# Routing the first layer's tokens in three groups instead of two, between the last attention tiles

## What is computed

```python
h = _layernorm(x) * (1 + ca) + sa
x = x + ga * _L0_attn_ref(h, ...)              # causal softmax attention, per batch
h = _layernorm(x) * (1 + cb) + sb
# _L0_ffn_ref:
logits = x_flat @ router_w.T                    # N = 2048 rows, E = 8 experts
chosen_e = argmax(softmax(logits)); chosen_p = max(softmax(logits))
pos = cumsum(onehot(chosen_e), axis=0)[row, chosen_e] - 1     # place in its expert's queue
kept = pos < C                                  # C = 384
buf[chosen_e, pos] += x_flat * kept             # rows scattered into expert slots
h = gelu(buf @ w1 + b1); eo = h @ w2 + b2       # per expert
y = eo[chosen_e, pos] * (chosen_p * kept)       # gathered back
x = x + gb * y
```

## Time and profile before

| | us |
|---|---|
| median of 3 runs | 942.2 (939.58 to 942.33) |
| the profiled execution: time | 943.0 |
| its span, first to last instruction | 941.3 |
| PE busy | 900.4 (96%) |
| ACT busy | 642.7 (68%) |
| DVE busy | 580.4 (62%) |
| POOL busy | 307.0 (33%) |
| mean granted clock of PE, of full speed | 0.98 |

### The profile page before, as it was taken

One profiled execution on the slowest core, in us unless ns is written; L12 is line 12 of the kernel. 1 busy time (PEld: TensorE's weight loads), 2 busy tenths in 40 slices (PEclk: granted clock), 3 DMA queues, 4 the chain that ended last, 5 costly groups with the idle time before them and its releaser, 6 DMA issues.

```text
span 941.3 us, 25419 instructions
## 1 busy us (share of the span) xinstructions
PE 900.4 (96%) x10209; PEld 662.7 (70%) x10209; DVE 580.4 (62%) x1348; ACT 642.7 (68%) x1094; POOL 307.0 (33%) x393
## 2 busy tenths in 40 slices
PE   8999995599999999999999999999999999999988
PEld 5687684366777777767777777767677776777777
DVE  5557011685666666666666666666666666667795
ACT  3552332487788787887878788787887878787343
POOL 4233802533423223241423223232424232325220
PEclk9998898799999999999999999999999999999999
DMA  8400622100020002002000200110020002000001
GB/s 238 163 2 23 198 99 56 31 2 2 2 94 2 3 6 90 2 2 94 2 3 1 94 3 1 58 38 2 2 94 1 2 2 42 2 2 2 1 12 34
DMA packets 27128, 35.48 MB, mean 38 GB/s; under 512 B 6042, under 2 KB 21716, under 8 KB 26836
## 3 DMA queue, kind: packets, MB, share of 16 engines
q1 hardware_dynamic: 25988, 31.76, 10.2%
q0 software_dynamic: 1024, 2.10, 0.8%
HBM read 28.48 MB, written 5.37 MB: 36 GB/s over the span
## 4 chain that ended last, share of the span: by engine, by line
PE 88%; DVE 5%; issue 2%; ACT 2%; DMA 1%; POOL 1%; SPq 0%; DVEq 0%; ACTq 0%; POOLq 0%
PE CX L444 24%; PE SC L407 19%; PE PT L427 15%; PE MI L388 6%; PE MI L386 3%; PE CX L463 2%; PE SC L1667 2%; PE PT L1678 2%; PE SC L1762 2%; PE SC L1528 1%; PE CX L1776 1%; PE MI L463 1%; PE SC L1444 1%; PE PT L1538 1%; PE MI L1551 1%
## 5 line engine op out<-in xcount | busy, mean ns | idle before, releaser
L566 DVE CUSTOM_DVE_ANT_0 soft<-SC,strips 128x1024 f32<-128x1024 f32 x256 | 303.3, 1222 | 76.8 <-PE SC L407 76.8
L527 ACT ACTIVATE soft<-soft,nmax 128x1024 f32<-128x1024 f32 x256 | 294.2, 1150 | 1.9 <-DVE nmax L566 1.9
L444 PE MATMUL CX<-PTs,V 128*64 128x256 f32 x2048 | 246.2, 383 | 0.0
L512 ACT COPY PTs<-PT 128x1024 f32<-128x1024 f32 x128 | 129.6, 1013 | 134.7 <-PE PT L427 134.7
L407 PE MATMUL SC<-qk 64*128 64x512 f32 x1536 | 209.5, 404 | 3.2 <-DVE nmax L566 1.5
L444 PEld LDWEIGHTS CX<-PTs,V 128*64 128x64 f32 x2048 | 143.3, 137 | 93.3 <-issue 36.1
L427 PEld LDWEIGHTS PT<-ident,soft 64*128 64x128 f32 x4096 | 158.5, 138 | 68.0 <-issue 28.2
L574 DVE COPY PTs<-PT 128x512 f32<-128x512 f32 x128 | 88.6, 692 | 159.8 <-PE PT L427 159.8
L427 PE MATMUL PT<-ident,soft 64*128 64x64 f32 x4096 | 175.6, 225 | 2.7 <-ACT PTs L512 2.4
L407 PEld LDWEIGHTS SC<-qk 64*128 64x128 f32 x1536 | 135.8, 186 | 27.3 <-issue 1.9
L613 POOL TENSOR_TENSOR x<-x,wo_out 128x256 f32<-128x256 f32 x64 | 47.5, 742 | 206.8 <-DVE wo_out L583 206.8
(11 more groups left out here) (281 smaller groups left out, 991.5 us busy)
## 6 DMA issues: line engine op xcount, KB each, us to landing
strips<-bias_vec SPq DMA_DIRECT2D x8, 1920.0 KB, 8.6
arena<-in_L_ffn_w SPq DMA_DIRECT2D x1, 2048.0 KB, 12.3
slots_in<-arena SPq DMA_DIRECT2D x1, 1536.0 KB, 8.6
arena<-slots_in SPq DMA_DIRECT2D x8, 192.0 KB, 3.7
slots_out<-arena SPq DMA_DIRECT2D x8, 192.0 KB, 2.1
x<-in_L_attn_x SPq DMA_DIRECT2D x2, 512.0 KB, 4.3
out<-x SPq DMA_DIRECT2D x4, 256.0 KB, 2.3
arena<-in_L_wmod SPq DMA_DIRECT2D x2, 384.0 KB, 5.3
```

The costliest lines, as they stand in the source:

```text
L444: ins = pe.matmul(CX[hd * DK:(hd + 1) * DK, 0:2 * P], V1[:, vb, t, hd * DK:(hd + 1) * DK], PTs[:, g % 2, hd, t, :], start=(t == 0), stop=( ...
L512: act.copy(turned_out(n, 0), turned_in(0)).then_inc(ev("ptA_out"), 1)
L527: act.activation(soft[:, n % RING, hd, :], soft[:, n % RING, hd, :], ACT.Exp, bias=nmax[:, j:j + 1], scale=-1.0, accum_out=rsum[:, hd, n % ...
L566: dve.tensor_tensor_reduce(soft[:, n % RING, hd, :], SC[hd][:, :], strips[:, u // B % 2, hd, i * P:i * P + S], 1.0, 3.4e38, ALU.add, ALU.m ...
```

## The change

The router works in three groups, tiles 0 to 7, 8 to 11 and 12 to 15 (`group`), and each has its own logits, choice, ranks, slot numbers and scatter. The order of attention tiles becomes 0 to 7, then 11 to 8, then 15 to 12, so that group 1 is complete after place 11; places 8 to 15 have widths 4, 3, 2, 1, 8, 7, 6, 5. Group 0's choice, ranks and slot numbers are written between the last attention places. POOL modulates group 0's rows in 16 operations of one tile each, where it used two of eight tiles. DVE modulates groups 1 and 2, each behind other work. Banks are reassigned, the last two attention places are written out of the loops, and PE's filler is 16 and 6 dummies (before 16, 5 and 6) and the 30 ahead of the experts, as before.

```diff
-        vec_banks = [PT[0], SC[0][:, 0:512], PT[1], SC[1][:, 0:512]]
+        vec_banks = [PT[0], PT[1], SC[0][:, 0:512], SC[1][:, 0:512]]
...
+
+        logit_banks = [SC[1][:, 0:64], SC[0][:, 0:32], MI[:, 0:32]]
+        rank_banks = [SC[1][:, 64:128], SC[0][:, 64:96], CX[:, 0:32]]
...
+        def group(g):
+
+            return (tiles(0), quarter(2), quarter(3))[g]
...
-        order0 = list(range(TB)) + list(range(NT - 1, TB - 1, -1))
+        order0 = list(range(TB)) + [11, 10, 9, 8] + [15, 14, 13, 12]
...
-                return four_sc[(3, 1, 0, 2)[k]]
+                return four_sc[(0, 1, 3, 1)[k]]
...
-            link(pool.tensor_tensor(rows_mod[:, tiles(0), :], rows0[:, tiles(0), :], bc_tiles(mod[:, 0, 0, 2, :], TB), ALU.mult))
-            link(pool.tensor_tensor(rows_mod[:, tiles(0), :], rows_mod[:, tiles(0), :], bc_tiles(mod[:, 0, 0, 1, :], TB), ALU.add))
+            for t in range(TB):
+                ins = pool.tensor_tensor(rows_mod[:, t, :], rows0[:, t, :], mod[:, 0, 0, 2, :], ALU.mult)
+            link(ins)
+            for t in range(TB):
+                ins = pool.tensor_tensor(rows_mod[:, t, :], rows_mod[:, t, :], mod[:, 0, 0, 1, :], ALU.add)
+            link(ins)
             pool.wait_ge(ev("slots_zeroed"), 16)
             scatter(0)
-            pool.wait_ge(ev("rows_mod_ready"), 1)
-            scatter(1)
+            for g in (1, 2):
+                pool.wait_ge(ev("rows_mod_ready"), g)
+                scatter(g)
...
-                if i == 14:
-                    norm_out(1, (0,))
+            turned0(NT - 4)
+            norm_out(1, (0,))
+            exp0(NT - 2)
+            turned0(NT - 3)
+            exp0(NT - 1)
+            turned0(NT - 2)
+            norm_out(1, (1,), (0,))
+            turned0(NT - 1)
...
-                if j % TB == TB - 1:
+                if j in (7, 11, 15):
                     link(ins)
-                    norm_variance(1, j // TB)
+                    variance_of(group((7, 11, 15).index(j)))
...
+            def group_rows(g):
+
+                link(tt(rows_mod[:, group(g), :], rows0[:, group(g), :], bc_tiles(mod[:, 0, 1, 2, :], 4), ALU.mult))
+                tt(rows_mod[:, group(g), :], rows_mod[:, group(g), :], bc_tiles(mod[:, 0, 1, 1, :], 4),
+                   ALU.add).then_inc(ev("rows_mod_ready"), 1)
+
+            def group_norm(g):
+
+                dve.wait_ge(ev("var_ready"), batches_until(1, g))
+                inverse_roots(group(g))
...
-            for i in range(4, NT):
+            for i in range(4, NT - 1):
+                if i == 13:
+                    dve.wait_ge(ev("inverse_ready"), 1)
+                    rows_out(tiles(0), rows0)
...
-                if i == 12:
-                    dve.wait_ge(ev("inverse_ready"), 1)
-                    rows_out(tiles(0), rows0)
+            stats0(NT - 5)
+            group_norm(1)
+            added0(NT - 4)
+            biased0(NT - 1)
+            router_choice(0)
+            rows_out(group(1), rows0)
+            slot_places(0)
+            added0(NT - 3)
             stats0(NT - 4)
-            router_choice(0)
-            added0(NT - 3)
             stats0(NT - 3)
+            dve.wait_ge(ev("h_ready"), 7)
+            dve.wait_ge(ev("mod0_ready"), 1)
+            group_rows(1)
             added0(NT - 2)
             stats0(NT - 2)
-            slot_places(0)
             added0(NT - 1)
             stats0(NT - 1)
-            dve.wait_ge(ev("var_ready"), batches_until(1, 1))
-            inverse_roots(tiles(1))
-            rows_out(tiles(1), rows0)
-            dve.wait_ge(ev("h_ready"), 8)
-            dve.wait_ge(ev("mod0_ready"), 1)
-            link(tt(rows_mod[:, tiles(1), :], rows0[:, tiles(1), :], bc_tiles(mod[:, 0, 1, 2, :], TB), ALU.mult))
-            tt(rows_mod[:, tiles(1), :], rows_mod[:, tiles(1), :], bc_tiles(mod[:, 0, 1, 1, :], TB), ALU.add).then_inc(ev("rows_mod_ready"), 1)
+            group_norm(2)
+            rows_out(group(2), rows0)
             router_choice(1)
             slot_places(1)
-            for b in range(B):
-                slot_weights(b)
+            router_choice(2)
+            slot_places(2)
+            dve.wait_ge(ev("h_ready"), 8)
+            group_rows(2)
+            for g in range(3):
+                slot_weights(g)
...
-            def logits0(b):
-
-                bank = (PT[1], MI)[b]
-                pe.wait_ge(ev("hT_ready"), 4 + 2 * b + 2)
-                if b == 0:
-                    pe.wait_ge(ev("pt0_out"), 12)
...
+                bank, some = logit_banks[g], group(g)
+                pe.wait_ge(ev("hT_ready"), 6 + g)
+                if g < 2:
+                    pe.wait_ge(ev("nmax0"), NT - 1 + g)
...
-                else:
+                pe.wait_ge(ev("hot_ready"), g + 1)
+                if g == 2:
                     pe.wait_ge(ev("att0_out"), NT)
...
-            for i in range(4, NT + 3):
-                if i < NT:
-                    scores0(i)
-                if 5 <= i < NT + 2:
+            for i in range(4, NT - 1):
...
                     turn0(i - 2)
-                if i >= 5:
                     context0(i - 3)
-                if i == 13:
-                    turn_rows(1, 0)
-                    turn_rows(1, 1)
-                if i == 15:
-                    logits0(0)
-                if i == 17:
-                    ranks0(0)
+            pe.wait_ge(ev("nmax0"), NT - 2)
+            turn_rows(1, 0)
+            turn_rows(1, 1)
+            turn0(NT - 3)
+            context0(NT - 4)
+            logits0(0)
+            pe.wait_ge(ev("hT_ready"), 6)
+            scores0(NT - 1)
+            turn0(NT - 2)
+            context0(NT - 3)
+            turn_rows(1, 2)
+            ranks0(0)
+            turn0(NT - 1)
+            context0(NT - 2)
+            context0(NT - 1)
+            logits0(1)
             def bias_columns(k):
 
...
             bias_columns(1)
-            keep_clock(four_sc[3], 16)
-            pe.wait_ge(ev("vec_ready"), 2)
-            turn_rows(1, 2)
-            keep_clock(four_sc[3], 5)
+            pe.wait_ge(ev("att0_out"), NT - 1)
+            keep_clock(CX, 16)
             turn_rows(1, 3)
-            keep_clock(four_sc[3], 6)
-            logits0(1)
+            keep_clock(CX, 6)
+            logits0(2)
             ranks0(1)
-            pe.wait_ge(ev("slot_numbers"), 1)
+            ranks0(2)
+            pe.wait_ge(ev("slot_numbers"), 2)
             bias_columns(2)
             bias_columns(3)
...
             pe.wait_ge(ev("scattered"), 16 * NT)
-            pe.wait_ge(ev("slot_numbers"), 2)
+            pe.wait_ge(ev("slot_numbers"), 3)
```

More of the change, by code:

```diff
@@ L751, in inverse_roots, with scatter @@
                 ins.then_inc(ev("inverse_ready"), 1)
-            def scatter(b):
-                pool.wait_ge(ev("slot_numbers"), b + 1)
-                for t in range(b * TB, b * TB + TB):
+            def scatter(g):
+                pool.wait_ge(ev("slot_numbers"), g + 1)
+                for t in range(group(g).start, group(g).stop):
                     pool.indirect_dma_start(slots_in, bass.IndirectOffsetOnAxis(ap=slot_s[:, t:t + 1], axis=0),
@@ L1581, in ranks0 @@
+                for t in range(some.stop):
+                    at = max(t - some.start, 0)
+                    mm(bank[:, at * E:], ones, hot1b[:, t:t + 1, :].to_broadcast([P, n - at, E]),
                        start=False, stop=False, skip_group_check=True)
[L1582 removed]
+                ins = mm(bank, before, hot1b[:, some.start + 1:some.stop + 1, :].rearrange("p t e -> p (t e)"), start=False, stop=True,
```

103 lines of the change are left out of this document (51 added, 52 removed).

## The result

| | us |
|---|---|
| before, median of 15 runs | 942.2 (939.58 to 943.07) |
| after, median of 15 runs | 945.06 (941.39 to 948.0) |
| ratio | 1.0036, 95% interval 1.0025 to 1.0048 |
| profiled execution of after | 947.21, span 945.5 (before 943.0, 941.3) |

What follows compares the result with a forecast made beforehand. Before, the scatter ended the stage; after, PE's own row of small work was to bound it. Slots 3.2 us later less 1.9 saved entering the experts gave +1.3, so 942.2 becomes 943.5, range 939.3 to 947.5.

Steps and rivals of the forecast that it cites:

- PE's own row: Group 2's ranks, bias, modulation and thirty dummies ahead of the experts: becomes the bound, ending at 110.3, +3.2 on 107.06.
- rival A: Clock falls in the attention's tail after PE's idle times, adding 1.5 and 1.7 us: 946.7, slower; chance 31%.
- Prices and the narrow places: Per-width costs in attention 0; narrow places 8 to 10 save PE 3.0 us ahead of batch 0's variance.
- The knot: Batch 0's eight row tiles ahead of wide place 13 in DVE's order: PE idles 2.5 us until 64.2.
- Slot numbers of batch 0: End of batch 0's router: 78.3 against 78.12 before, so moved up in order but not in time.
- the last addition: End of DVE's additions for the last attention places: 81.8 against 78.65 before, +3.1.
- The sixteen dummies: PE's dummies after group 0's bias matmuls: 3.6 us at 2.4 GHz or 5.2 as before, ending 86.5 or 88.1.
- Group 1's ranks: Queued behind group 2's logits on PE, ending 89.7 or 91.3; DVE waits 1.6 to 3.2 us for them.
- POOL: Idle 2.7 to 4.3 us between its two scatter blocks; last issue ends at 102.1 or 103.7, against 103.09.
- The warm entry: PE enters the experts straight from its dummies without the idle 1.60, saving 1.9 us in the first block.
- the 1.7 us in the thirty dummies: Extra cost in the dummies ahead of the experts if the clock comes back only there.
- Rival C: POOL's tile-wise operations hold DVE's root chain of group 1, ending about 71; at most 0.5 added: 944.0; chance 5%.

Runs made afterwards that it cites:

- yardstick: The changed kernel itself run once more with no edit, on a slow chip; 952.71 against 948.73 for before, ratio 1.0042.
- ranks first: After, with group 1's ranks moved ahead of group 2's row transposes, six dummies and logits in PE's order; 949.35, ratio 1.0007 to before.
- knot: After, with place 13's biased step moved ahead of batch 0's eight row tiles in DVE's order; 949.52, ratio 1.0005 to before.
- best: After, with place 13 ahead of the rows, fewer dummies, group 1's ranks earlier and modulation vectors as filler; 944.4 against 948.73, ratio 0.9948 to before.
- best, again: A second run of the version with all four edits to after, on the same slow chip; 943.37 against 949.21 for before, ratio 0.9946.
- after, 14 dummies: After, with 14 in place of 30 dummy matmuls ahead of the experts; 948.61 against 949.41 for before, ratio 0.9995.
- after, filler: After, with 9 and 8 dummy matmuls put into PE's two idle times in the attention's tail; 950.65, ratio 1.0017 to before.
- before, 14 dummies: The kernel before, with 14 in place of 30 dummy matmuls ahead of the experts; 949.21, ratio 1.0002 to before.

## Why the prediction was right, and where its working was not

The forecast was 943.5 with 939.3 to 947.5, most of the chance on a difference under 0.3%. The median came out 1.5 us above it, within the range and just over the edge of what was called the same (0.36%). The direction and the bound were right: PE's own row replaces the scatter, as the chain shows, and no profile of the changed kernel or its variants has PE waiting for the slots. The size was not: +1.3 us forecast, +2.9 measured, and the forecast's ratio of 1.0014 lies outside the interval of 1.0025 to 1.0048. The forecast's own range, 941.5 to 945, just misses the median; the stated range holds it because rival A stretches it to 947.5.

- **Prices and the narrow places.** Batch 0's variance was forecast at 55.5 and came at 55.08; roots done at 59.6, came at 59.2. Right.
- **The knot.** PE idle 2.5 us until 64.2 forecast; 2.27 until 63.83 measured. Its removal moved the tail by 1.9 us.
- **Slot numbers of batch 0.** 78.3 forecast, 79.36 measured; the last addition 81.8, measured 83.3. The steps were right, their clock was not: in 65.5 to 68.5 and 79 to 82 it was 0.50. Against the yardstick, which had the full clock there, each of the two stretches cost 1.4 us, at row transposes, transposes and contexts. (Two of the sums on the way were 0.2 too high each: 71.6 and 4.07 make 75.7, and 75.9 and 2.2 make 78.1.)
- **The sixteen dummies.** Forecast from 82.9 to 88.1 at the latest, measured from 85.4 to 90.7. Their own time was priced right (5.2, the slow end I took); it is their start that was 2.5 late, and 2.4 of it was there when the last contexts ended (82.7 in place of 80.3). This is the term that was too small, and what it left out is the lower clock in the attention's tail, which the forecast put at nothing and only rival A priced. Group 1's ranks ended at 93.8 and not 91.3, and DVE's wait for them was 4.32 in place of 3.2.
- **POOL.** Gap forecast 2.7 to 4.3, measured 4.86. The last issue was to end at 103.7 and ended at 105.5.
- **PE's own row.** From the one-hot to the end of the dummies I counted 15.4 us at the lower clock and 0.85 more. It took 16.3 (96.35 to 112.63). So the row was priced right and began 2.3 us late: slots at 112.63 against 110.3.
- **The warm entry.** 1.9 forecast, 1.7 measured.
- **Rival A**, the clock falling in the attention's tail, is what the profiled execution shows, at 31% of the chance and 946.7 where that execution took 947.2. It priced the fall behind PE's second idle time; there was one behind the first, too. The closeness of the sum is luck: of its terms the 1.7 us in the thirty dummies did not come (7.00 us against 6.86), and the two falls together cost 2.8 where 1.5 was taken. On another chip the tail kept the full clock and the ratio was the same, since the row waited there for something else. On the chip where before takes 942, the kernel with group 0's rows in two operations, otherwise after, had one such stretch and not two, and its profiled execution took 944.9. Of the fifteen executions of after the fastest (941.4) has the highest mean granted clock, 0.983, and the two slowest (947.9 and 948.0) 0.974. So the clock explains the profiled 4.2 against 1.3 and part of the spread; how much of the median's 2.9 it is is not shown.
- **Rival C** was seen in part: DVE's chain took 0.85 us more and ended at 69.6, where I had it end at about 71, and DVE had no scores before 73.1, so that nothing of it reached the time. The Trainium skill, "SBUF — State Buffer", Who interferes with whom, limits the blocking to DVE instructions with two SBUF inputs or in a two-port mode. The rows agree for L1090 and L1091. L1087 and L1088 have one input and took 0.38 as well; they are tensor_scalar, which that section names among the operations that can enter a two-port mode. Whether they ran in it no run here shows.

The three engines form a circle: group 1's ranks, behind group 2's logits in PE's list, hold DVE, which holds group 2's one-hot, which holds PE's row. The working had it (91.3, 92.5, 94.0), and its steps came out as counted: 93.8, 94.9, 96.35. Through this circle the late start of the dummies reached the term I summed from. I forgot it only afterwards, in the expectation for the kernel with the ranks first, which took the start of the row as fixed.

## What to carry to other kernels

When a serial stage is split into more rounds, each round adds a hand-over between engines; look at the order in which the most loaded engine's list takes the new rounds, and let each round's answer stand directly behind the input it needs. Cut filler where its engine is the bound and leave it where the engine waits: the same cut of sixteen dummies was worth some 2 to 4 us in one kernel and nothing that shows in the other, and the kernel that waits became 0.2% slower when the dummies further ahead were cut and the modulation vectors moved. Whether real work that is due later (here two modulation vectors) is the better filler was not tested by itself.

## What the hardware showed that was not expected

**Releases held up behind a block of scatters.** On the two slower chips, in eight of nine profiles, an engine that waited for PE got its release 2.5 to 4.1 us late. The hold-up ended 2.4 to 2.7 us after the start of POOL's last scatter issue of the first block; the transfer behind the last issue of before took 2.2 us.

| kernel | PE had ended (us) | POOL's last issue starts | waiting engine goes on |
|---|---|---|---|
| after, again | 87.5 | 89.17 | ACT 91.55 |
| knot | 85.6 | 87.24 | ACT 89.63 |
| best | 85.9 | 86.73 | DVE 89.15 |
| best, again | 86.0 | 86.77 | DVE 89.23 |
| after, 14 dummies | 89.3 | 89.75 | ACT 92.30 |
| after, filler | 89.6 | 89.61 | ACT 92.13 |
| after, ranks first | 89.2 | 89.52 | DVE 92.23 |
| before, 14 dummies | 87.6 | 88.36 | ACT 90.83 |

In the kernel with the ranks first PE itself paused in that time, ahead of transposes for which the profile shows no wait (0.54, 0.45 and 0.98 us). In the kernel with 4 dummies for 16 ACT was released at once (88.60), 1.4 us before POOL's last issue, and DVE at 92.67, when PE had just ended. Where before takes 942 no such wait shows in any of five profiles, one of them the kernel without the first block. The last line of the table is the slowest execution of its kernel (953.1, the fastest 947.1). Its slots came at 113.64 in place of 107.06; of these 6.6 us the hold-up is 3.2, and the lower clock 3.1 (6.60 against 5.27 in the sixteen dummies, 3.58 against 1.85 in the logits). How much of the spread of before on these chips is the hold-up's, one profile can't say. What holds the releases is open. The one run that could have told, without the scatters, fell on a chip without the effect.

**The first scatter next to DVE.** Group 0's first issue takes 1.72 us after the change, 1.24 before and 1.24 again for the first issue of the kernel without the first block, which starts at 94.47 without a modulation of DVE beside it. In after it starts at 80.27, and DVE modulates group 1's rows from 80.20 to 81.60, with two SBUF inputs. But DVE's modulation of group 2's rows (98.23 to 99.66), the same two operations, runs beside issues that take 0.96 and 1.01 us. So the neighbour alone does not make an issue longer, and what makes the first one longer is open.

**The lower clock comes and goes between executions.** In the profiled execution of after PE had 1.2 GHz in three stretches between 61 and 90 us. The yardstick, the same code with the same idle times, had it in none; the first two lines are its windows. The knot's kernel had none either, though PE idles 2.22 us right ahead of the stretch in the third line, nor had the two best runs up to 85 us, with the same idle time. The other six variants had one stretch between 61 and 87 us, of under 4 us: five at 77 to 82, behind the idle time of 1.96, and the one with filler in both idle times at 84.

```profile
65.50:68.50 3.00, 2.90 (x27) 2.69 (x26) 2.44 (x11) 2.92 (x4) 2.98 (x8) 1.00 0.02 5
77.00:81.00 4.00, 4.00 (x45) 3.87 (x43) 3.27 (x14) 1.47 (x2) 1.44 (x1) 1.00 0.00 0
```
```profile
74.60:84.00 9.40, 9.40 (x77) 7.72 (x78) 7.61 (x38) 2.64 (x4) 5.16 (x5) 1.00 0.09 29
```

So what one profile says of the clock holds for one execution.
